# A decoder layer on one core: both halves of x in one slot, and the second norm's rows turned behind the out projection

## What is computed

```
x  = layernorm(x + attention(x))            # 16 heads of 128, 4 key/value heads, rotary, window of 128
x  = layernorm(x + cross(x, ctx))           # x times a softmax matrix that depends on ctx alone
x  = layernorm(x + moe(x))                  # 2 shared + 16 routed experts of 176, top 4 of 16
```

## Time and profile before

| | us |
|---|---|
| median of 3 runs | 411.34 (411.28 to 411.34) |
| the profiled execution | 409.84 |
| its span, first to last instruction | 408.0 |
| mean granted TensorE clock in it | 0.996 |
| busy: TensorE, VectorE, ScalarE, GpSimd | 388.0, 284.2, 266.7, 179.3 |

### The profile page before, as it was taken

How to read it: one execution, slowest core, us unless ns; L and a number is a source line. 1 busy time by engine, 2 the same in 40 slices (tenths; PEclk the granted TensorE clock), 3 DMA queues, 4 the chain that set the end, 5 groups by cost and what they waited for, 6 DMA issues and landing times.

```text
span 408.0 us, 8463 instructions
## 1 busy us (share of the span) xinstructions
PE 388.0 (95%) x2559; PEld 346.7 (85%) x2559; DVE 284.2 (70%) x797; ACT 266.7 (65%) x669; POOL 179.3 (44%) x314
## 2 busy tenths in 40 slices
PE   6976999999999999989999989999999999999995
PEld 3666898998888999879999868889989998999994
DVE  2786998886785886877878767477659545744445
ACT  3668997776767685767767677565775744444352
POOL 0243775554664643764463765486956300000000
PEclk9998999999999999999999999999999999999999
DMA  6711421000000000000000099223222222343221
GB/s 200 273 53 53 152 81 28 3 0 2 1 2 27 0 0 0 0 0 0 0 0 0 11 278 332 80 79 93 86 83 85 93 59 78 85 149 100 86 66 51
DMA packets 24677, 28.25 MB, mean 69 GB/s; under 512 B 2961, under 2 KB 17194, under 8 KB 24650
## 3 DMA queue, kind: packets, MB, share of 16 engines
q1 hardware_dynamic: 24650, 27.92, 22.3%
HBM read 26.80 MB, written 1.11 MB: 68 GB/s over the span
## 4 chain that ended last, share of the span: by engine, by line
PE 75%; ACT 9%; DVE 9%; issue 5%; DMA 1%; SPq 1%; ACTq 0%; DVEq 0%
PE bank L704 20%; PE bank L706 20%; PE bank L705 20%; PE bank L834 4%; PE bank L843 3%; PE bank L833 2%; PE bank L806 2%; ACT probs L1089 2%; PE bank L800 1%; ACT probs L1087 1%; ACT swapped L1081 1%; ACT xln L1098 1%; DMA ctx_sb<-in_ctx 1%; PE bank L907 1%; DVE pT_lo L1226 1%
## 5 line engine op out<-in xcount | busy, mean ns | idle before, releaser
L1020 ACT ACTIVATE hid<-bank,b_cols 128x512 f32<-128x512 f32 x48 | 32.9, 686 | 55.6 <-PE bank L706 47.1
L1243 DVE TENSOR_TENSOR hid<-hid,gate_rows 128x512 f32<-128x512 f32 (+1 forms) x44 | 31.9, 724 | 47.7 <-ACT hid L1020 47.5
L1601 POOL TENSOR_SCALAR nprobs<-probs,rsums 128x128 f32<-128x128 f32 x64 | 23.8, 373 | 75.3 <-DVE rsums L1362 66.9
L705 PE MATMUL bank<-w_lo,hid_hi 128*128 128x256 f32 (+1 forms) x200 | 56.3, 282 | 0.0
L1593 POOL TENSOR_TENSOR queryT<-by_cos,by_sin 128x512 f32<-128x512 f32 x32 | 41.1, 1283 | 26.4 <-DVE by_sin L1347 25.4
L1080 ACT COPY swapped<-bank 64x512 f32<-64x512 f32 x40 | 23.3, 583 | 33.1 <-PE bank L706 32.8
L1226 DVE TENSOR_TENSOR hid_lo<-hid,hid_hi 128x512 fp32r<-128x512 f32 x48 | 36.1, 753 | 5.4 <-ACT hid_hi L1041 5.4
L704 PE MATMUL bank<-xT_hi,wq_hi 128*128 128x256 f32 x128 | 38.4, 300 | 1.3 <-issue 1.2
L705 PEld LDWEIGHTS bank<-w_lo,hid_hi 128*128 128x128 f32 (+1 forms) x200 | 37.7, 188 | 2.1
L706 PE MATMUL bank<-x2T_hi,w_lo 128*128 128x512 f32 (+1 forms) x100 | 39.4, 394 | 0.0
L834 PE MATMUL bank<-keyT,queryT 128*128 128x256 f32 x128 | 38.8, 385 | 0.0
(11 more groups left out here) (177 smaller groups left out, 1236.5 us busy)
## 6 DMA issues: line engine op xcount, KB each, us to landing
gate_rows<-gates_d SPq DMA_DIRECT2D x16, 256.0 KB, 3.2
stage<-in_L_attn_q_kernel SPq DMA_DIRECT2D x4, 512.0 KB, 6.6
stage<-in_L_attn_out_kernel SPq DMA_DIRECT2D x4, 512.0 KB, 3.6
w_raw<-in_L_ffn_routed_w SPq DMA_DIRECT2D x2, 1024.0 KB, 9.9
gate_rows<-gates_d SPq DMA_DIRECT2D x8, 224.0 KB, 3.1
gate_rows<-gates_d SPq DMA_DIRECT2D x8, 192.0 KB, 2.8
gate_rows<-gates_d SPq DMA_DIRECT2D x8, 160.0 KB, 2.5
w_raw<-in_L_ffn_routed_w SPq DMA_DIRECT2D x2, 528.0 KB, 7.7
```

What stands on the lines that cost most here:

```text
L705: nc.tensor.matmul(o, sh, ml, start=False, stop=False, **kw)
L1020: nc.scalar.activation(hid[:, u % 2, :], z_bank[u % 3][:], ACT.Relu, bias=b1_cols[:, i % NC:i % NC + 1]).then_inc(relu_done, 1)
L1243: nc.vector.tensor_tensor(own, own, gate_rows[rows, i % 3, :], ALU.mult).then_inc(gated, 1)
L1601: nc.gpsimd.tensor_scalar(nprobs[:, u, 0:W], probs[:, u, 0:W], rsums[:, u, 0:1], 1.0, ALU.mult, ALU.mult)
```

## The change

x0 and x1 become one slot x: four transposes fill one bank, one cast of 128 x 512 and one subtraction read it. There are 17 slots then, and their banks alternate as before up to q7; y is put into bank 1 by name (`bank_of`), so that x, in bank 0, has another bank than the y ahead of it, and `freed_count` looks for the last slot in the same bank. y is due at 29.3, behind out0 of group 1 on TensorE. The same number moves y on the two other engines to 13.05:

```diff
--- before.py
+++ after.py
@@ -73,9 +73,9 @@
 
 
 
-SLOT_AT = {"x0": -2.5, "x1": -2.5, "q0": -1.25, "k0": -1, "q1": -0.75, "q2": -0.5, "q3": 1.75,
+SLOT_AT = {"x": -2.5, "q0": -1.25, "k0": -1, "q1": -0.75, "q2": -0.5, "q3": 1.75,
            "k1": 2.75, "q4": 4.75, "v1": 5.5, "v0": 6.5, "q5": 7.25, "q6": 7.75, "q7": 11,
-           "n": 25.5, "m0": 26.5, "m1": 26.75, "y": 29.25}
+           "n": 25.5, "m0": 26.5, "m1": 26.75, "y": 29.3}
 WINDOW = -2.5
 
 
@@ -169,14 +169,20 @@
     return NSLOT * turn - len(LATE) + SLOTS.index(s) + 1
 
 
+def bank_of(s):
+
+    return 1 if s == "y" else SLOTS.index(s) % 2
+
+
 def freed_count(b, s):
 
     turn, n = b + (s in LATE), SLOTS.index(s)
     if isinstance(turn, int):
-        before = [i for i, (_, other) in enumerate(FILLS[:slot_count(b, s) - 1]) if (n - SLOTS.index(other)) % 2 == 0]
+        before = [i for i, (_, other) in enumerate(FILLS[:slot_count(b, s) - 1]) if bank_of(other) == bank_of(s)]
         return before[-1] + 1 if before else 0
 
-    return NSLOT * turn - len(LATE) + max(n - 1, 0)
+    back = [k for k in range(1, NSLOT) if bank_of(SLOTS[n - k]) == bank_of(s)][0]
+    return NSLOT * turn - len(LATE) + n - back + 1
 
 
 def rope_count(b, s):
@@ -605,7 +611,7 @@
 
             def load_next_x(b):
 
-                sp.wait_ge(projected, slot_count(b, "x1"))
+                sp.wait_ge(projected, slot_count(b, "x"))
                 sp.dma_start(xb[:], x[bass.ds(b + 1, 1)].rearrange("a (t p) c -> p (a t) c", p=P)).then_inc(ld_xb, 16)
 
             load_next_x(0)
@@ -785,14 +791,16 @@
 
             def slot(b, s):
 
-                n, kind, j = SLOTS.index(s), s[0], int(s[1:] or 0)
-                o = proj_bank[n % 2]
+                kind, j = s[0], int(s[1:] or 0)
+                o = proj_bank[bank_of(s)]
                 if not (isinstance(b, int) and freed_count(b, s) == 0):
                     e.wait_ge(emptied, freed_count(b, s))
                 if kind == "x":
                     e.wait_ge(ld_xb, 16 * (b + 1))
-                    for t in range(TT):
-                        mm = nc.tensor.transpose(o[:, t * P:(t + 1) * P], xb[:, t, j * P:(j + 1) * P], ident[:])
+                    for k in range(KC):
+                        for t in range(TT):
+                            mm = nc.tensor.transpose(o[:, k * T + t * P:k * T + (t + 1) * P],
+                                                     xb[:, t, k * P:(k + 1) * P], ident[:])
                 elif kind in "ny":
                     e.wait_ge(ln_done, 2 * b + (1 if kind == "n" else 2))
                     for k in range(KC):
@@ -815,7 +823,7 @@
                 else:
                     wh, wl = (wk_hi, wk_lo) if kind == "k" else (wq_hi, wq_lo)
                     e.wait_ge(w_lo, piece_count("k" if kind == "k" else f"q{j // 2}"))
-                    e.wait_ge(emptied, slot_count(b, "x1"))
+                    e.wait_ge(emptied, slot_count(b, "x"))
                     for a in range(2):
                         for k in range(KC):
                             f = slice((2 * j + a) * D, (2 * j + a + 1) * D)
@@ -1058,13 +1066,13 @@
                                              scale=ln_rstd[:, t:t + 1]).then_inc(x3_by_act, 1)
 
             def slot(b, s):
-                n, kind, j = SLOTS.index(s), s[0], int(s[1:] or 0)
+                kind, j = s[0], int(s[1:] or 0)
                 if kind in "nm":
                     return
-                o = proj_bank[n % 2]
+                o = proj_bank[bank_of(s)]
                 e.wait_ge(projected, slot_count(b, s))
                 if kind == "x":
-                    nc.scalar.copy(xT_hi[:, j, :], o[:, 0:T]).then_inc(split_hi, 1)
+                    nc.scalar.copy(xT_hi[:], o[:].rearrange("p (k t) -> p k t", k=KC)).then_inc(split_hi, 1)
                 elif kind == "y":
                     e.wait_ge(w_lo, len(PIECES))
                     e.sem_inc(act_passed, 1)
@@ -1333,7 +1341,7 @@
                 if kind in "xv":
                     e.wait_ge(split_hi, split_count(b, s))
                     if kind == "x":
-                        low(xT_lo[:, j, :], o[:, 0:T], xT_hi[:, j, :]).then_inc(emptied, 1)
+                        low(xT_lo[:], o[:].rearrange("p (k t) -> p k t", k=KC), xT_hi[:]).then_inc(emptied, 1)
                     else:
                         low(v_lo[:, j, :], o[:], v_hi[:, j, :]).then_inc(emptied, 1)
                     return
```

## The result

The changed kernel takes 415.48 us (median of 7 runs, 412.93 to 417.15), the kernel before 411.34 (7 runs, 410.55 to 411.89): the ratio is 1.0088, with a 95% interval of 1.0065 to 1.0112. Slower, as forecast, but by 4.1 us (0.9%) instead of 2.2, and outside the range of 411.8 to 414.9. The seven runs lie over 4 us, where the kernel before lies over 1.3; their mean granted clocks are 0.981 to 0.992. The profiled execution is one of the slower ones: 416.22, span 414.4, clock 0.981, against 409.84, 408.0 and 0.996. It is 6.4 longer, more than the medians are apart.

The account below looks back on a forecast made before the run. TensorE, busy 95% of the span, was taken to bound the kernel. 0.51 (turn 1) + 1.08 (q0, turns 2 and 3) + 0.62 (end) = 2.2 us, forecast 413.5 against a median of 411.34; range 411.8 to 414.9.

Parts of the forecast that it names:

- parts 1 and 2: Turns 2 and 3: TensorE's waits at y and x go and return as one 2.0 us wait at q0.
- part 2: ScalarE's and VectorE's moved orders queue y's and x's subtractions behind a delayed chain: q0 0.54 us later per turn.
- at least 1.5: Sign in the profile after: on VectorE, y's subtraction comes at least 1.5 us after y's cast.
- The size at q0 in turns 2 and 3: q0 starts 0.54 us later in each of turns 2 and 3: 1.08 in all, ends 0.5 and 1.5.
- Turn 1: x in one slot: its cast needs all four transposes, so q0 comes 0.51 us later, ends 0.23 and 0.70.
- The end: Behind the loop, y's subtraction delays the centroid copy, weight split and up_top: plus 0.62 us, ends 0.46 and 0.8.
- rival C: Slower still: TensorE's clock falls after the new idle spells, 1.0 us each, one to three times: 414.5 to 416.5; chance 0.07.
- The sum of stalls: Turn 1, q0 in turns 2 and 3, and the end: 0.51 + 1.08 + 0.62 = 2.2 us.
- Rival A: Faster: TensorE's two waits go and nothing replaces them, q0 1.45 us sooner in turns 2 and 3: 409.6; chance 0.07.
- Rival B: No change: the stalls are made good later in the turn, the n slot's wait could go: 412.0; chance 0.13.

Follow-up runs that it names:

- e4: The changed kernel with ScalarE and VectorE kept in their old orders, so that only TensorE's order changes: 413.99 us, ratio 1.0070 to the kernel before.
- e1: The changed kernel with y also due at 29.3 on ScalarE, so its cast comes behind heads_hi1: 409.42 us, ratio 0.9957 to the kernel before.
- e2: The changed kernel with y due at 29.25 as before, leaving only x in one slot with its own bank: 411.08 us, ratio 0.9998.
- e3: The kernel before with only y's due time moved to 29.3, x still in two slots: 416.81 us, ratio 1.0138.
- e6: The changed kernel with 7 unread matmuls ahead of q0 in turns 1 to 3 and 9 ahead of up_top: 414.22 us, ratio 1.0060.
- e5: The changed kernel with 7 unread matmuls ahead of q0 in turns 1 to 3: 414.14 us, ratio 1.0072 to the kernel before.
- e10: The changed kernel run and profiled once more, nothing altered: 415.16 us, ratio 1.0084 to the kernel before.

## Why the prediction was wrong

- **Direction and mechanism of the stalls** (parts 1 and 2): right. The waits at y and x went, and one longer wait at q0 took their place; VectorE idles, then does heads_lo1, y, x. y's subtraction comes 1.72 behind y's cast, "at least 1.5" was asked for.
- **Which order is to blame** (part 2): half wrong. I named the moved due times of ScalarE and VectorE. e4 has the old ones and q0 is no earlier. What counts is two things together: heads_hi1 stands behind y on ScalarE, as it did before (e1 undoes this and q0 comes 0.96 sooner), and y now comes late on TensorE (e2 leaves it early and q0 comes at 5.09).
- **The size at q0 in turns 2 and 3**: 0.54 forecast, 0.33 measured. y and q0's last step came as worked out (1.67, 0.74). From a cast's start to its subtraction I took the 0.74 of y's pair; heads and x took 0.63 and 0.62. y's cast came 0.82 behind its transposes, not 0.88, and x's subtraction 0.59 behind y's, not 0.64.
- **Turn 1**: 0.51 forecast, 0.34 measured, by the same step (0.62 for 0.74) and by 0.64 to the cast instead of 0.69. The part belongs to the merge: from x to q0 in turn 1 it is 2.00 in e2, with one slot, and 1.67 in e3, with two.
- **The end**: 0.62 forecast, 0.44 measured; the order of pieces was as forecast, and the split followed the centroid copy by 0.26 (0.25 before), so that copy and not the weights' landing released it.
- **The step that failed is rival C.** The sum of stalls, 2.2, was too large by 0.75; with the measured 1.45 it would have given 412.8, inside the range. The clock, left out of the sum with a chance of 0.07, was worth more than all the stalls: some 2 us in the median, by e6. The reason I gave, that the new idle spells are "single and lie between dense stretches", was no reason: the two spells of before, 0.67 and 0.36 with an out projection between them, had been merged by the change into one of 1.85. e1, e5, e6 and the tally under e10 show that the falls in the loop go with that wait. The price was too low too: 1.0 per fall, from the 2 us of the earlier trace rows alone, where the profiles show about 1.5. With the measured 1.45 and one to two falls the forecast would have been 414.3 to 415.8. That the measured 415.48 lies in rival C's own 414.5 to 416.5 is partly luck, as its stalls were too large and its price too small.
- **Rival A** (409.6) did not happen, but e1 came to 409.4 by another path than A thought of: q0 still waits 0.89. **Rival B**: from q0 to the last value matmul turn 1 took as long as before to 0.04, and the n slot's wait, which was to go, was 0.29, 0.39 and 0.18, so nothing was given back.

## What to carry to other kernels

An operation that fills a wait on the bounding engine also delays whatever is queued behind the thing it overtakes; follow that thing through the in-order queues of the other engines before moving it, and move there what doesn't depend on it (heads_hi1 ahead of y: from +0.9% to -0.4%). One long wait can be dearer than two short ones with work between, when the long one lets TensorE's clock fall; a wider spread of the runs is a sign of it (4.2 us against 1.3 here). A wait is only worth filling with work that nothing covers itself with: look at the next rotation or cast that hangs on the pieces pushed back.

## What the hardware showed that I had not expected

In the changed kernel a single wait of 1.85 us on TensorE, between stretches at over 90% busy, was followed by a fall of the granted clock from 1.00 to 0.50 in two of two turns of one profile and in one of two turns of another; waits of 0.89 in e1 were not followed by one in its profile. Nor was the wait of 2.32 at `up_top` in either profile of the changed kernel, so the length of the wait alone does not decide it; what else does is not shown. A fall behind q0 cost about 1.5 us. In a dense stream the same subtraction of 512 columns started 0.62 to 0.63 behind its cast's start for heads and x, and 0.74 behind it for y; why y's pair is slower was not tried.
